# Where VectorE takes the second layer norm's statistics of the last three groups, and when GpSimd forms their residual

## The reference

```
x = x + tanh(g_xattn) * cross_attention(layernorm(x), ctx)      # 16 heads of 8, keys masked by seq_len, plus a bias
h = layernorm(x)                                                # eps 1e-5, no scale or shift
scores = softmax(h @ gate_w.T + gate_b);  the two best of 8 experts per row, val_sum = sum of their scores
for each expert e:
    inter = h @ wi.T + bi + (h @ lora_A[e].T) @ lora_B[e].T     # 128 -> 512, LoRA rank 16
    out  += count_e * val_sum * (relu(inter) @ wo.T + bo)
x = x + tanh(g_ffn) * out
```

## Time and profile before

| | |
|---|---|
| time, median of 3 runs | 278.7 us (277.4 to 281.32) |
| the profiled execution | 275.81 us, span 274.0 us |
| TensorE (matmul) busy | 245.4 us, 90% of the span |
| VectorE busy | 211.0 us, 77% |
| ScalarE busy | 163.0 us, 59% |
| GpSimd busy | 163.7 us, 60% |
| the chain that ended last, by engine | PE 54%, DVE 26%, ACT 5%, POOL 5%, issue 5% |

### The profile page before, as it was taken

One profiled execution on the slowest core, in us unless ns is written; L12 is line 12 of the kernel. 1 busy time (PEld: TensorE's weight loads), 2 busy tenths in 40 slices (PEclk: granted clock), 3 DMA queues, 4 the chain that ended last, 5 costly groups with the idle time before them and its releaser, 6 DMA issues.

```text
span 274.0 us, 8038 instructions
## 1 busy us (share of the span) xinstructions
PE 245.4 (90%) x2966; PEld 184.0 (67%) x2966; DVE 211.0 (77%) x618; ACT 163.0 (59%) x319; POOL 163.7 (60%) x311
## 2 busy tenths in 40 slices
PE   0358979899999999989999999999999999999995
PEld 0235556565666566656567689797887889897865
DVE  5778777899999999997948777869596858585432
ACT  5878785888888888896877552424233342423230
POOL 6888676687878776686895549392919050505110
DMA  4759997747776866640000000101010101000011
GB/s 116 196 136 208 218 210 203 189 107 205 177 221 147 211 154 160 151 69 6 8 6 2 4 0 0 39 2 38 2 38 0 42 0 38 2 16 22 7 33 38
DMA packets 48461, 23.46 MB, mean 86 GB/s; under 512 B 7680, under 2 KB 48296, under 8 KB 48424
## 3 DMA queue, kind: packets, MB, share of 16 engines
q1 hardware_dynamic: 47520, 22.77, 34.8%
q10 hardware_dynamic: 904, 0.19, 0.4%
HBM read 7.29 MB, written 2.10 MB: 34 GB/s over the span
## 4 chain that ended last, share of the span: by engine, by line
PE 54%; DVE 26%; ACT 5%; POOL 5%; issue 5%; DMA 2%; ACTq 1%; POOLq 0%; DVEq 0%
PE bank L1106 19%; DVE negmax L1317 12%; PE bank_max L1141 9%; PE bank L1016 6%; PE bank L1048 6%; DVE rest L1268 3%; PE bank L1083 3%; PE bank L1099 2%; PE bank L1059 2%; PE bank L1022 2%; DMA b_rows<-in_L_xattn_b_dram 2%; DVE hsum L1440 2%; DVE u L1432 2%; ACT stack L764 2%; ACT probs L813 1%
## 5 line engine op out<-in xcount | busy, mean ns | idle before, releaser
L1317 DVE TENSOR_REDUCE negmax<-bank 128x4 f32<-128x512 f32 x128 | 83.3, 678 | 10.0 <-PE bank L1016 9.8
L813 ACT ACTIVATE probs<-bank 128x512 f32<-128x512 f32 x128 | 71.8, 602 | 14.7 <-PE bank L1022 13.5
L1016 PE MATMUL bank<-stack 64*128 64x128 bf16 x512 | 52.1, 235 | 8.9 <-DVE negmax L1317 5.5
L1016 PEld LDWEIGHTS bank<-stack 64*128 64x128 bf16 x512 | 31.6, 101 | 30.8 <-DVE negmax L1317 18.9
L1106 PE MATMUL bank<-u_part,b_part 128*128 128x512 f32 x192 | 51.9, 398 | 0.1
L853 ACT ACTIVATE h<-bank,bi_col 128x512 f32<-128x512 f32 x32 | 22.1, 690 | 48.5 <-PE bank L1106 48.5
L1022 PE MATMUL bank<-stack 64*128 64x128 bf16 x512 | 48.7, 222 | 0.7 <-issue 0.4
L1440 DVE SCALAR_TENSOR_TENSOR hsum<-bank,nbi_col,h 128x512 f32<-128x512 f32 x32 | 23.7, 748 | 24.6 <-PE bank L1106 24.6
L1048 PE MATMUL bank<-probs,vpad 128*32 128x128 f32 x1024 | 41.9, 282 | 0.0
L1106 PEld LDWEIGHTS bank<-u_part,b_part 128*128 128x128 f32 x192 | 35.5, 188 | 8.2 <-ACT h L853 0.5
L648 POOL TENSOR_TENSOR x_part<-KV,x_part 128x512 fp32r<-128x512 f32 x8 | 10.4, 1301 | 50.9 <-ACT x_part L835 50.9
(11 more groups left out here) (135 smaller groups left out, 409.8 us busy)
## 6 DMA issues: line engine op xcount, KB each, us to landing
stack<-part SPq DMA_DIRECT2D x96, 128.0 KB, 3.0
KV<-in_ctx_dram SPq DMA_DIRECT2D x5, 512.0 KB, 4.5
X<-in_x_dram SPq DMA_DIRECT2D x7, 256.0 KB, 4.8
out_dram<-res SPq DMA_DIRECT2D x7, 256.0 KB, 2.3
KV<-in_ctx_dram SPq DMA_DIRECT2D x5, 256.0 KB, 5.6
stack<-bias_line SPq DMA_DIRECT2D x7, 48.0 KB
stack<-max_rows SPq DMA_DIRECT2D x13, 24.0 KB
X<-in_x_dram SPq DMA_DIRECT2D x2, 128.0 KB, 2.3
```

Of the source, the lines that this page charges most:

```text
L813: act.activation(probs[:, i % 4, :], sc2[i % 2][:, :], ACT.Exp).then_inc(s_exp, 1)
L1016: mm = pe.matmul(sc1[i % 2][:, j * 128:(j + 1) * 128], stack[at, s, h0 + 2 * j, q0:q0 + 128], stack[at, s, h0 + 2 * j, 512 + q0:640 + q0], ...
L1317: dve.tensor_reduce(negmax[:, p % 2, n % 2, 8 * (u // 2) + u % 2:8 * (u // 2) + u % 2 + 7:2], bank_cols(sc1[i % 2]), AX.X, ALU.max, negate ...
```

## The change

In groups 0 to 2 of the expert loop, VectorE takes the statistics of group g + 5 between sum 1 and sum 2 of group g, and no longer at the end of the group. GpSimd forms `residual(g + 5)` as the first instruction of group g, ahead of `x_low(g + 1)` and `make_base(g)`, and no longer behind them. No instruction is added or taken away.

```diff
@@ GpSimd
             for g in range(GROUPS):
+                if g + 5 < GROUPS:
+                    residual(g + 5)
                 if g + 1 < GROUPS:
                     x_low(g + 1)
                 make_base(g)
-                if g + 5 < GROUPS:
-                    residual(g + 5)
                 if g + 4 < GROUPS:
                     rsqrt2(g + 4)
                     normalise2(g + 4)
@@ VectorE
                 if g == 0:
                     mask_u(1)
                 sum_experts(g, 1)
+                if g + 5 < GROUPS:
+                    for k in range(3):
+                        stats2_of(g + 5, k)
                 sum_experts(g, 2)
                 sum_experts(g, 3)
                 if g + 1 < GROUPS:
@@
                     gates_end(g + 2)
-                if g + 5 < GROUPS:
-                    for k in range(3):
-                        stats2_of(g + 5, k)
```

## The result

The changed kernel takes 275.46 us (median of 10 runs, 274.38 to 276.46), the kernel before 277.37 (10 runs, 276.37 to 281.32). The ratio is 0.9945, with a 95% interval of 0.9923 to 0.9967: faster by about 1.5 us (0.9 to 2.1), clear of no change but a small step, under 2%. The ratio leaves out 281.32, a run in the chip's slower state; the two medians lie 1.9 us apart, which is inside that interval. A second set gave 0.9946.

What follows compares the result with a forecast made beforehand. TensorE, busy 90% of the span, was taken to wait for VectorE's sum 0 in three groups: 0.46 + 0.45 + 0.46 = 1.37 us gain, holds costing 0 to 0.2. From the 278.7 median: 277.3 us, range 275.2 to 280.3.

Steps and rivals of the forecast that it cites:

- gates held for longer than the margin: Rival, chance 0.14: GpSimd's sum holds VectorE's gates beyond the margin, gain only 0.8 to 1.2 us, 277.7 us.
- The wait on sum 0: TensorE ahead of `first_expert(g, 3)`: waits 0.36 us for VectorE's sum 0, three times; removing it gains 1.37 us.
- The margin of 0.12 us: Sum 0 behind group 0: 0.90 us margin plus 0.19 from `tie`, less 0.97 for held `score`; in time, barely.
- The holds: VectorE beside GpSimd: `score` about 1.2 us in group 0, 0.7 in group 1; `veps2` 0.7 to 0.9 in group 0.
- the page's sum of 1.3 us: By the Trainium skill's full-instruction block: first hold 1.15 us instead of 0.97, 0.06 us wait left, gain 1.3 instead of 1.37.
- The instruction at 145.59: VectorE 128x4 addition taking 1.43 us against 0.19: held 1.24 us, to about 1.1 us behind the start of GpSimd's sum.
- the aggregates at 124.66: Four VectorE aggregates, 0.37 us together, read as entirely beside a GpSimd subtraction of 1.27: so `bn_aggr` is not held.
- The cover between sums 1 and 2: VectorE idle 1.34 us ahead of sum 2: the statistics' 1.26 us fit with 0.07 to spare, cost nothing.
- the slack of 0.90 us: VectorE between sums 2 and 3: statistics may take about 0.9 us longer before TensorE sees it at `out_weights`.
- The rival that ends slower: Chance 0.07: `veps2` waits for successive GpSimd instructions, `out_weights` late in groups 0 to 2; 1.6 us slower, 280.3 us.
- That the sum into `X` would come late: Rival: `stats2_of` waits for GpSimd's sum; group 6's would have to be 7 us late; given no chance of its own.

Runs made afterwards that it cites:

- e8: Kernel before, with GpSimd's sums into X formed one group ahead and statistics still at the end of the group: ratio 0.9980, expert part 118.78 us.
- e3: Changed kernel with GpSimd's sums into X formed one group ahead, past VectorE's gates: ratio to the kernel before 0.9929, expert part 117.49 us.
- e6: Changed kernel with GpSimd's sums of groups 5 to 7 cut into four instructions each: ratio to the kernel before 0.9963, expert part 117.44 us.
- e4: Changed kernel with eight more bn_stats, results unused, between sums 1 and 2 of groups 0 to 2: ratio to the kernel before 1.0005.
- e1: Changed kernel with GpSimd's sum put back behind make_base, only the statistics moved: ratio to the kernel before 1.0162, expert part 123.02 us.
- e5: Changed kernel with the statistics between sums 2 and 3 instead of 1 and 2: ratio to the kernel before 1.0007, expert part 118.88 us.
- e2: Kernel before with only GpSimd's sum moved to the head of a group, statistics left at its end: ratio 1.0095, expert part 120.50 us.

## Why the prediction was right

The predicted 277.3 us lies 1.8 above the measured 275.46, inside the range, whose lower end of 275.2 is 0.3 us away. Of that, 1.3 us is the base: the three runs shown before had a median of 278.7, ten have 277.37. The other 0.5 is the gain, 1.37 us forecast against 1.9 between the medians. That the number came inside is owed to the width of the range as much as to the sum.

The mechanism is judged better by the gain in the profile, which was 1.17 us: 0.31, 0.46 and 0.42 by turns, against the forecast 0.46, 0.45 and 0.46. That is right in kind and 0.2 us too large, and it lies where the prediction put its rival of gates held for longer than the margin (0.8 to 1.2 us). In the first turn this rival came true in small. By the runs (1.5 us, 0.9 to 2.1) forecast and rival can't be told apart.

- **The wait on sum 0 is what bounded the turn.** Shown: the step of 1.74 us is 1.42 and 1.37, the chain runs through TensorE alone, and e8 keeps the old turns with the statistics where they were.
- **The margin of 0.12 us was mis-sized.** Removing the statistics was taken to bring sum 0 forward by 1.26 us. It brought 1.14. VectorE in order of time, before:

```profile
173.21 0.15 DVE L1417 TENSOR_TENSOR lsum<-top 128x4 f32<-128x4 f32 x1
...
173.51 0.22 DVE L1423 TENSOR_SCALAR gate<-lsum,tanh_g 128x4 f32<-128x4 f32 x1
173.64 0.86 DVE L1344 BATCH_NORM_STATS2 stats<-X 128x6 f32<-128x128 f32 x4
...
174.90 0.76 DVE L1432 TENSOR_TENSOR u<-bank,hot 128x256 f32<-128x256 f32 x2
```

The statistics started 0.13 us after the start of `gate`, overlapping its end, and `mask_u` followed 1.26 us later, 1.39 after `gate`. Now `mask_u`, which waits for the gates to be complete, comes 0.25 us after `gate` (174.50 to 174.75). With that and a hold of 1.03 instead of 0.97 us the margin is 1.14 - 0.36 + 0.19 - 1.03 = -0.06, and TensorE waits 0.02 to 0.05 us. The rest of the 0.16 by which the first turn exceeds 14.34, some 0.12 us, is lost behind the wait (0.81 instead of 0.69 us to the next row). e3 and e6 give both back. A clean turn is 14.33 to 14.38 us, so taking 14.34 for all three was up to 0.04 short as well.
- **The holds.** `score` 1.22 and 0.60 us against about 1.2 and 0.7; `veps2` 0.83 in group 0 against 0.7 to 0.9, and `out_weights` of group 0 in its place. By the Trainium skill (SBUF — State Buffer, the section on the two separate sides), a held instruction waits for the whole of the other. Here `score`, which takes 0.19 us alone, ended at 170.90 with GpSimd's sum at 170.85, so it was let go 0.14 us before that sum's recorded end. The hold of 1.03 us lies nearer to the prediction's reading from the row (0.97) than to the page's (1.15). That the page's sum of 1.3 us came nearer to the profile's 1.17 is luck: its hold was too long, and the missing 0.12 us of the margin was in neither.
- **Two rows were misread**, without harm. The instruction at 145.59 takes 0.15 us alone (173.21 above) and not 0.19, so the sum let it go 1.13 us behind its start, not 1.1. And the aggregates at 124.66 ran beside GpSimd's subtraction for 0.03 us only, as it ended at 124.69; the row says nothing on whether `bn_aggr` is held. The changed profile does: four of them took 0.36 us at 164.16, all inside GpSimd's 164.08 to 165.37.
- **The cover between sums 1 and 2.** Right: nothing was lost, though `veps2` made sum 2 late in group 0. e4 found its edge: 1.54 us more cost 0.46 us per group, with the slack of 0.90 us that the prediction had.
- **The rival that ends slower** (GpSimd's instructions hand the lock to each other) did not come: `veps` at 164.56 got through between two of them, in all three groups, and `score` between two pieces in e6. Its price for a late sum 3 was of the right kind, as e1, e4 and e5 show. What decides who gets through when both wait, as at 145.59, was not tried.
- **That the sum into `X` would come late** was given nothing, rightly for this kernel; e1 shows that it is the first thing to go wrong when only one half is made.

## What to carry to other kernels

Before work is moved out of a late chain, measure the hole that it goes into and the slack behind it: the same instructions won 1.2 us in a hole of 1.34 us and nothing in the next one of 0.8. Move its producer with it. And where GpSimd runs an instruction with two SBUF inputs, look at what small VectorE instructions stand beside it: held in a chain without slack each costs its hold, and cutting or shifting the GpSimd instruction cures it.

## What the runs showed of the hardware

- A VectorE addition of a constant to 128x4 elements, 0.17 us when nothing holds it, took 0.83 and 1.09 us beside GpSimd instructions with two SBUF inputs (164.56 after, 176.59 in e2).
- In eight such holds the VectorE instruction, less what it takes alone, was let go 0.13 to 0.15 us before the recorded end of the GpSimd instruction: 18.09 and 145.59 before; 164.56, 169.68, 178.88 and 184.16 after; 170.47 and 176.59 in e2.
- Beside GpSimd's normalisations (128x128, one SBUF tensor in, 0.80 us each) holds were short. `tie` at 169.98 before, `score` at 185.71 in e3 and `veps` at 167.04 in e5 were let go 0.29 to 0.30 us after the start of such an instruction, and `score` at 169.54 before, which came 0.44 us into one, was not held. `veps` at 181.52 in e4, 0.11 us into one, was not held either; why is open.
- Four `bn_stats` (163.38 after, 0.86 us) and four `bn_aggr` (164.16, 0.36) beside GpSimd instructions with two SBUF inputs took as long as with GpSimd idle (173.64 before: 0.86 and 0.36) and were not held, nor was the sum of a PSUM and an SBUF tensor (164.62 before, 0.75 us, beside GpSimd's 163.91 to 165.19).
- A hold can make the next: in e2 a hold of 1.04 us was followed by one of 0.92, since the queue now met a GpSimd instruction that it had missed by 0.4 us before (`veps` over at 174.99, `x_low` from 175.40).
- Behind a wait of at most 0.05 us the next three matmuls of TensorE took 0.12 us more (0.81 instead of 0.69, 176.88 and 191.32 after); behind one of 0.36 they took 0.10 more (0.79, 177.03 before).
